# A one-core decoder layer: the loops of TensorE, VectorE, ScalarE and GpSimd written out in all three stages

## What is computed

```python
# 1: linear attention
Xn = _layernorm(X, ln_g, ln_b)
QKV = jnp.einsum('bsd,ed->bse', Xn, W_in)
Q, K, V = jnp.split(QKV, 3, axis=-1)
Q = _rotary(Q, ROT); K = _rotary(K, ROT)
A = jnp.sum(_l2norm(K) * V, axis=-2)
Y = A[:, None, :] * _l2norm(Q)
Y = jnp.einsum('bsd,ed->bse', Y, W_out); return Y + X
# 2: cross attention, 16 heads of 64; keys are the context's 64 rows and the latents' own 64
w = jnp.einsum('bhqd,bhkd->bhqk', q * scale, k * scale)
w = jax.nn.softmax(w.astype(jnp.float32), axis=-1).astype(q.dtype)
out = jnp.einsum('bhqk,bhkd->bhqd', w, v); return out @ Wo
# 3: mixture of 8 experts, the 2 best of each token
probs = jax.nn.softmax(jnp.einsum('bsd,de->bse', x, Wg) + bg, axis=-1)
topk_vals, topk_idx = jax.lax.top_k(probs, TOP_K)
h = jax.nn.gelu(jnp.einsum('bsd,edf->besf', x, W1) + b1[None, :, None, :], approximate=False)
y = jnp.einsum('besf,efd->besd', h, W2) + b2[None, :, None, :]
out = jnp.einsum('bse,besd->bsd', probs, y)
```

## Time and profile before

| | us |
|---|---|
| median of 3 runs | 1647.21 |
| lowest and highest | 1641.94 and 1647.63 |
| profiled execution: span from first to last instruction | 1682.3 |
| busy in it: TensorE, VectorE, ScalarE, GpSimd | 1437.9, 1337.9, 973.4, 971.4 |

### The profile page before, as it was taken

One profiled execution on the slowest core, in us unless ns is written; L12 is line 12 of the kernel. 1 busy time (PEld: TensorE's weight loads), 2 busy tenths in 40 slices (PEclk: granted clock), 3 DMA queues, 4 the chain that ended last, 5 costly groups with the idle time before them and its releaser, 6 DMA issues.

```text
span 1682.3 us, 41166 instructions
## 1 busy us (share of the span) xinstructions
PE 1437.9 (85%) x10381; PEld 1230.8 (73%) x10381; DVE 1337.9 (80%) x5130; ACT 973.4 (58%) x3763; POOL 971.4 (58%) x1485
## 2 busy tenths in 40 slices
PE   4689999999999999999999999999997498988950
PEld 3478787877777777878777777778885498988840
DVE  4478988888888898888888888988876577766757
ACT  2266666666656665666666566666664255544535
POOL 2355665666666666666666666666644245544458
PEclk7599999999999999999999999999998699999975
DMA  3000000000000000000000000000000666766647
GB/s 82 11 11 7 14 18 15 15 14 13 15 15 15 15 13 13 17 14 15 13 15 13 15 14 15 13 15 16 8 11 15 189 217 208 223 191 199 203 132 214
DMA packets 89529, 95.40 MB, mean 57 GB/s; under 512 B 12137, under 2 KB 75756, under 8 KB 89282
## 3 DMA queue, kind: packets, MB, share of 16 engines
q1 hardware_dynamic: 69714, 71.97, 14.8%
q0 software_dynamic: 8896, 17.20, 3.0%
q10 hardware_dynamic: 10800, 5.06, 1.2%
HBM read 71.88 MB, written 23.35 MB: 57 GB/s over the span
## 4 chain that ended last, share of the span: by engine, by line
DVE 37%; issue 25%; ACT 15%; PE 15%; DMA 3%; another core or an unknown queue 2%; POOL 1%; DVEq 1%; SPq 1%; ACTq 0%; POOLq 0%
ACT probs L622 14%; DVE neg_max L767 7%; DVE pT L779 3%; PE ps_t L1419 3%; DVE k_pick L824 2%; DVE x1s L854 2%; PE ps_u L1419 2%; DVE turned L810 2%; DVE l_hat L871 2%; DVE yT L834 1%; PE ps_a L1381 1%; DVE top_atf L950 1%; DVE st_z L845 1%; DVE st_x L862 1%
## 5 line engine op out<-in xcount | busy, mean ns | idle before, releaser
L622 ACT ACTIVATE probs<-ps_s,neg_max 128x128 f32<-128x128 f32 x1024 | 362.6, 366 | 433.2 <-DVE neg_max L767 432.2
L508 POOL TENSOR_TENSOR probs_n<-probs,inv_sum 128x512 f32<-128x512 f32 x256 | 265.5, 1037 | 150.7 <-DVE inv_sum L773 148.6
L1265 PEld LDWEIGHTS ps_s<-kvT,u_sb 128*128 128x128 f32 x2048 | 255.3, 192 | 48.7 <-issue 44.9
L1265 PE MATMUL ps_s<-kvT,u_sb 128*128 128x128 f32 x2048 | 281.5, 281 | 3.2 <-issue 3.2
L1278 PE MATMUL ps_o<-value_w,tT 128*128 128x128 f32 x2048 | 261.8, 276 | 2.7 <-ACT tT L633 2.2
L1298 PE MATMUL ps_t<-pT,kv_rows 128*128 128x512 f32 x512 | 262.3, 594 | 0.8 <-DVE pT L779 0.8
L1278 PEld LDWEIGHTS ps_o<-value_w,tT 128*128 128x128 f32 x2048 | 244.7, 192 | 6.8 <-ACT tT L633 4.1
L570 POOL DMA_INDIRECT y_rows<-wvT,f_id x144 | 146.4, 1017 | 169.9 <-DVE wvT L1179 124.9
L520 POOL DMA_INDIRECT x_rows<-routed,pos_i x128 | 136.3, 1065 | 132.0 <-DVE pos_i L1003 100.3
L1313 PE MATMUL ps_u<-lT_hi,score_hi 128*128 128x256 f32 x512 | 184.5, 360 | 27.4 <-DVE lT_lo L893 21.1
L622 ACT ACTIVATION_READ_ACCUMULATOR probs<-ps_s,neg_max 128x1 f32 x1024 | 207.6, 203 | 0.0
(11 more groups left out here) (246 smaller groups left out, 3453.2 us busy)
## 6 DMA issues: line engine op xcount, KB each, us to landing
u_sb<-in_expert_w SPq DMA_DIRECT2D x45, 578.0 KB
tT<-in_expert_w SPq DMA_DIRECT2D x27, 578.0 KB
f_x<-x_rows SPq DMA_DIRECT2D x72, 130.0 KB
tT<-y_rows SPq DMA_DIRECT2D x32, 256.0 KB, 3.7
x_raw<-in_x SPq DMA_DIRECT2D x64, 64.0 KB, 1.8
c_raw<-in_ctx_in SPq DMA_DIRECT2D x128, 32.0 KB, 2.0
out<-u_sb ACTq DMA_DIRECT2D x16, 256.0 KB, 3.0
y_rows<-wvT,f_id POOLq DMA_INDIRECT x144
```

The source lines that it names most:

```text
L508: nc.gpsimd.tensor_tensor(probs_n[:, sl], probs[:, sl], inv_sum[:, sl, :].rearrange("p (u o) -> p u o", o=1).to_broadcast([P, UP, P]), ALU ...
L622: last = nc.scalar.activation(probs[:, sl, j], ps_s[sl][:, j * P:(j + 1) * P], ACT.Exp, bias=neg_max[:, sl, j:j + 1], accum_out=sums[:, sl ...
L1265: last = nc.tensor.matmul(ps_s[sl][:, j * P:(j + 1) * P], u_sb[:, c // 2, BT * p + b, h:h + 2].rearrange("p h s -> p (h s)"), kvT[:, c, 1 ...
```

## The change

`periods` no longer has a loop: all 74 periods are written out on every engine, SyncE among them. `turns` no longer has a loop either and is used by all engines in stages two and three; the old one lives on as `rolled_turns`, which SyncE alone uses for the expert tiles. No instruction that computes on data is added, removed or moved. What goes are the branches, the loop registers and the register arithmetic ahead of waits and addresses; what comes is a longer instruction stream for each engine.

```diff
         def periods(eng, period):
 
-            lo = 6
-            fours = (NT - 6 - lo) // 4
-            hi = lo + 4 * fours
-            for t in range(FIRST, lo):
+            for t in range(FIRST, LAST + 1):
                 period(t, t % 4)
-            with eng.Fori(0, fours) as i:
-                for step in range(4):
-                    period(i * 4 + (lo + step), (lo + step) % 4)
-            for t in range(hi, LAST + 1):
-                period(t, t % 4)
-
-        def turns(eng, n, step, by, tail=0):
+
+        def turns(n, step, by):
+
+            for i in range(n):
+                step(i, i % by)
+
+        def rolled_turns(eng, n, step, by, tail=0):
...
-            turns(sp, NF, ffn, W_RING, W_RING)
+            rolled_turns(sp, NF, ffn, W_RING, W_RING)
...
-            turns(sp, NZ, last_in, RING)
+            turns(NZ, last_in, RING)
...
-            turns(pool, NF, ffn, W_RING)
+            turns(NF, ffn, W_RING)
...
-            turns(dve, NF, ffn, W_RING, W_RING)
+            turns(NF, ffn, W_RING)
...
-            turns(pe, NF, ffn, W_RING, W_RING)
+            turns(NF, ffn, W_RING)
```

More of the change, by code:

```diff
@@ L583, in last @@
                     rstd(e_mv[:, o, :, 1], e_ve[:, o], e_rs[:, o], eps_ln, e_moments, ZT * g, e_eps, e_rstd, g - 1)
-            turns(pool, NZ, last, RING)
+            turns(NZ, last, RING)
             last(NZ, 0)
@@ L708, in _ @@
             upper_weights(0, 0)
-            turns(act, NF, ffn, W_RING, W_RING)
+            turns(NF, ffn, W_RING)
             def last(g, q):
@@ L720, in last @@
                               e_out[:, q % 2]).then_inc(s_out[q % 2], 16)
-            turns(act, NZ, last, RING)
+            turns(NZ, last, RING)
         @block.vector
@@ L1209, in last @@
                     nc.vector.scalar_tensor_tensor(e_nm[:, o], e_mv[:, o, :, 0], -1.0, e_rs[:, o], ALU.mult, ALU.mult).then_inc(e_nm_done, 1)
-            turns(dve, NZ, last, RING)
+            turns(NZ, last, RING)
             last(NZ, 0)
```

## The result

| | before | after |
|---|---|---|
| median | 1647.42 us (1641.94 to 1648.0, 4 runs) | 1604.34 us (1603.82 to 1608.02, 4 runs) |
| ratio, 95% interval | | 0.9749 (0.9729 to 0.9768) |
| the profiled execution | span 1682.3 us | 1608.02 us, span 1606.1 us |
| stretch between the first row maxima of periods 6 and 58 | 998.5 us | 959.6 us |
| 56 expert tiles, `f_id` to `f_id` | 233.0 us | 196.6 us |

The account below looks back on a forecast made before the run. The prediction took VectorE's in-order stream, with its hand-over to ScalarE's exponentials, to bound the looped periods. Gains of 30.8 + 0 + 0 + 0.9 + 0.5 = 32.2 us off 1647.2 gave 1615.0 us, range 1603 to 1631.

Parts of the forecast that it names:

- The 12 jumps: VectorE's jumps back between the 13 turns of the looped periods: 2.57 us each, 30.8 us gained by removing them.
- Register arithmetic: Register instructions in the looped periods: removing them gains 0, bounds 2 us of loss and 1 us of gain.
- the test by period 5: Written-out period 5 takes 18.64 us against 18.60 looped, taken to show that register arithmetic in the periods costs nothing.
- Late pieces of code: Fetching the longer straight stream of the periods: 0 cost expected, upper bound 18 us.
- The rival: Late pieces of code all along the written-out periods, leaving 18 us of gain, 1629 us; chance 0.10.
- What the others' jumps cost: Jumps of the other four engines in the periods: nothing beside VectorE's, which explain the whole lengthening of the period.
- The expert tiles: Jumps removed among the expert tiles: 0.9 us gained, bounds nothing to 26 us.
- the expert tiles fall to the written-out pace: Rival: looped expert tiles go from 4.16 to 3.69 us each, 26 us more gain, 1589 us; chance 0.08.
- The last sum: Two ordinary jumps removed in the last sum: 0.5 us gained, between 0 and 1.
- I assume that this distance stays: The profiled span's 35.1 us above the median of the runs was assumed to remain after the change.
- Slower by code among the tiles: Rival: code fetches come late among the expert tiles, where DMA engines are busy, costing 72 us, 1687 us; chance 0.05.

Follow-up runs that it names:

- E2: Kernel before with the periods written out on TensorE, ScalarE, GpSimd and SyncE, VectorE still looped; first chip: 1696.18 us, ratio 1.003.
- E1: Kernel before with the periods written out on VectorE alone, every other loop kept; first chip: 1650.34 us, ratio 0.9759.
- E7: Kernel before with VectorE's loop at eight periods a turn instead of four, six turns in place of 13; second chip: 1629.74 us, ratio 0.9908.
- E3: Kernel before with the periods written out on all five engines, loops over expert tiles and last groups kept; first chip: 1656.79 us, ratio 0.9799.
- E11: Changed kernel with two already met waits added on VectorE ahead of each period's first row maximum; third chip: 1605.16 us, ratio 0.974.
- E12: Kernel before with the periods written out on all engines but TensorE; third chip: 1610.02 us, ratio 0.9773.
- E4: Kernel before with only the expert tiles written out, on all engines but SyncE; first chip: 1663.03 us, ratio 0.9829.
- E10: Kernel before with only the expert tiles written out, on all engines but SyncE; third chip: 1643.02 us, ratio 0.9975.
- E9: Changed kernel unchanged, run again on the third chip: 1603.88 us, ratio 0.9733.
- E5: Changed kernel unchanged, run again on the second chip: 1604.31 us, ratio 0.976.
- E6: Changed kernel with SyncE's loop over the expert tiles written out too; second chip: 1603.48 us, ratio 0.9751.
- E8: Changed kernel with four no-operations meant for VectorE ahead of each first row maximum, which did not get into the program; second chip: 1605.19 us, ratio 0.9769.

## Why the prediction was right, and where it fell short

**The 12 jumps, 30.8 us: right.** Four readings agree: the row is gone after, it stays in E2, E1 brings 35.5 us on its own (with VectorE's register arithmetic in it), and E7 keeps 5 jumps and 13.1 us of it.

**Register arithmetic, 0: wrong, and the largest error.** The written-out period is 18.42 us (E3 and E11: 18.41), the looped one 18.61: 52 x 0.184 = 9.6 us. My bounds were 2 us of loss and 1 us of gain. That the range still held the result was luck: its lower end had 10 us of spread that was meant for the expert tiles and the runs. The step that failed is the test by period 5, the last before the loop. The row maximum that ends it already stands in VectorE's loop, and ahead of it TensorE enters its own loop, which makes the scores late. The runs tell the two shares apart: period 5 takes 18.50 us where VectorE alone is looped (E2), 18.56 where TensorE alone is (E12), and 18.64 with all. Period 4, in the same trace, is free of both. Its first row maximum:

```profile
153.66 0.69 DVE L767 TENSOR_REDUCE neg_max<-ps_s 128x4 f32<-128x512 f32 x1
```

With the 172.10 of the earlier trace rows that is 18.44 us, which would have told it. E1 shows that the gain belongs to VectorE: 18.37 us with it alone written out, while E2, with the rest written out, stays at 18.67.

Where in the period it lies is read, not isolated. Counted from the row maximum of one quarter to the next, a looped period goes 4.88, 4.38, 3.72, 5.62 us, a written-out one 4.87, 4.31, 3.73, 5.52: the loss is in the second quarter and in the fourth. The chain ahead of the row maximum that ends the second quarter, before:

```profile
372.05 0.29 DVE st_x L862
372.34 0.03 issue
372.37 0.02 DVEq L312
372.39 0.04 issue
372.43 0.07 DVE mv_x L867
372.50 0.05 issue
372.55 0.02 DVEq L766
372.57 0.04 issue
372.61 0.70 DVE neg_max L767
```

and after:

```profile
386.16 0.29 DVE st_x L859
386.45 0.03 issue
386.48 0.02 DVEq L312
386.50 0.04 issue
386.54 0.06 DVE mv_x L864
386.60 0.04 issue
386.64 0.70 DVE neg_max L764
```

From `st_x` to `neg_max` it is 0.56 us looped and 0.48 written out. The step ahead of `mv_x`, L312, is a wait for VectorE's own result, so the sequencer can't run ahead, and what it does next lies bare between two short instructions. "DVEq L766" is the wait for ScalarE's exponentials, which the changed kernel has too (L763). What is longer is the way to it: in the loop the trace has a register instruction of 0.04 us (L765) between `mv_x` and L766.

The fourth quarter loses its time at its very end, ahead of the first row maximum of the next period. Before, and after:

```profile
363.05 0.28 DVE L893 TENSOR_TENSOR lT_lo<-kvT,l_upper 128x128 fp32r<-128x128 f32 x1
363.35 0.69 DVE L767 TENSOR_REDUCE neg_max<-ps_s 128x4 f32<-128x512 f32 x1
```
```profile
358.78 0.28 DVE L890 TENSOR_TENSOR lT_lo<-kvT,l_upper 128x128 fp32r<-128x128 f32 x1
358.99 0.69 DVE L764 TENSOR_REDUCE neg_max<-ps_s 128x4 f32<-128x512 f32 x1
```

TensorE's scores come at the same point in both, 0.18 us behind the start of `lT_lo`, by the updates of their semaphore. From there to the row maximum it is 0.11 us looped (before, E2, E4, E10) and 0.02 written out (after, E1, E3, E9, E11, E12; the middle one of 51 periods each). What stands in the longer gap is a register instruction of 0.04 us (L766): it waits for the scores itself and works out the count of the next wait, and only then can the row maximum be issued. E1 and E12 have the short gap with TensorE looped, E2 the long one with TensorE written out, so it is VectorE's own.

"The arithmetic runs on the sequencers while the datapaths work" holds, by these rows, only where the sequencer is ahead of its engine; behind a wait that ends last the arithmetic lies bare. E11's waits stood ahead of the score wait and cost nothing. Not tried: the looped kernel with the two waits ahead of the row maximum exchanged, so that the arithmetic stands ahead of the scores.

**Late pieces of code, 0: right, nearly.** 52 x 18.423 = 958.0 us stand against 959.6 measured: 1.6 us, mostly in six periods of 18.6 to 18.8 us (26, 27, 37, 46, 48 and 49). They are the same six in E3, E5, E6, E8 and E9, and others in E11, where VectorE's stream has two instructions more a period. So they hang on the place in the stream. The rival had 14 us and an upper bound of 18. The price is this small though q8, the queue I had taken for TensorE's, now moves all the time. The queues from 340.6 to 414.3 us of the changed kernel, four periods:

```profile
q8 instruction: 4, 0.07, 0.4%
...
q14 instruction: 6, 0.05, 0.3%
```

Before, q14 had 5 packets in a turn and q8 stood still. So straight code on all engines costs in q14 about what one engine's loop cost. What differs, as I read it, is when: along a straight line the code is there before it is needed, behind a taken branch it is fetched only once the engine has got there. VectorE's branch before is at 418.18 us, the next packet of 8192 bytes starts at 419.2, and the next instruction (of registers) runs at 421.0. This is what the Trainium skill says in "Runtime: NRT & Kernel Launch", section "Instruction fetch mechanics"; the 2.8 us between the branch and the next instruction agree.

**What the others' jumps cost, 0: right with all removed, wrong by its reason.** I said the lengthening was all VectorE's. It was, because 0.3 to 0.4 us of TensorE's jump lay under 2.6 us. Take VectorE's alone and 4 to 5.4 us come up (E1, E12). The change removed both, so the sum was not touched; for the smaller change it would have been.

**The expert tiles, 0.9 us: right on two chips, far off on the first.** On the third chip, the time from the first scatter of rows to the last is 250.0 us with all written out (E9) and 251.7 with looped tiles (E12): 1.7 us. E10's gain against the kernel before is 5.0 us, of which 3.3 are not located, since no profile of the kernel before is from that chip. The rival "the expert tiles fall to the written-out pace" took 4.16 - 3.69 us a tile for an effect of the loop. The pace did fall to 196.6 / 56 = 3.51 us, but looped tiles run at 3.55 too. My own reason, that the waits by "remote" are no branch, held on the third chip, yet E4 shows up to 25 us of gain on a chip that has them.

**The last sum, 0.5 us:** it takes 62.0 us from the last tile's `f_id` to the end, 61.7 before. No gain can be seen.

**"I assume that this distance stays": wrong, without harm.** The 35.1 us between span and median were the expert tiles of a slower execution, most likely of another chip. The periods that carry the sum hardly differ (998.5 to 1000.8 us looped, in the profile before, E4 and E10; 958.8 to 959.6 written out, on all three chips), so a difference worked out in them could be taken over.

**Slower by code among the tiles: wrong.** The change's tiles take 3.51 us each at 243 GB/s and a DMA share of 0.80, and VectorE waits by "issue" there hardly at all.

The sum again, with what was measured: on the third chip the stretch gave 998.7 - 959.0 = 39.7 us (E10 to E9) and the tiles up to 5.0 (E10, whose last sum is looped). That makes 44.7 us where 44.1 were measured between medians (1647.98 - 1603.88). The 39.7 are the jumps, 31.0 in E10, where the forecast had 30.8; the register arithmetic, 52 x (18.609 - 18.411) = 10.3, forecast at 0; and the late pieces, 1.6 the other way: 31.0 + 10.3 - 1.6 = 39.7. In the first pair the stretch gave 38.9 of the 43.1 us; the other 4.2, where the forecast had 1.4, are not located.

## What to carry to other kernels

Look in the list of waits for "issue" rows whose count is the number of turns less one: there an engine fetches its own loop again, and the price is that of a jump (2.6 us here), not of an instruction, so a longer body with fewer turns buys part of it for less code (E7: 7 of 12 jumps, 16 of the 39 us of the stretch). Take jumps off the engine that all others wait for first, and expect the next engine's to come up from underneath (E1, E12). In a loop, look also for register arithmetic behind the wait that ends last: it cost some 0.09 us there, while two more instructions ahead of that wait cost nothing (E11). To test a loop against straight code take a written-out period that touches neither end of the loop, and compare like parts of a span (here 52 periods) when whole runs come from different chips.

## What the runs showed of the hardware that was not expected

- **Not each loop is fetched again.** VectorE's body of some 430 recorded instructions a turn was, with 5 packets a turn on q14; q8 stood still during TensorE's turns of some 1130 from the third turn on, and the jumps that remained in E1 and E12 cost 0.3 to 0.4 us.
- **The same looped tiles take 198.8 us on two chips and 236 to 242 on another** (E7 and E12 against E1 to E3; 233 in the profile before), in E3 and E12 with the same instruction counts, a granted clock of 0.98 against 1.00 and a DMA share of 0.65 against 0.79. The loss comes in stalls of about 2.5 us. Written-out tiles there take 220.4 us (E4). The cause is open.
- **Straight code is close to free:** 52 periods of it on all engines cost 1.6 us, with 62 more packets on q8 and 19 on q14 over the whole kernel.
- **Fewer jumps beside it made VectorE's no cheaper:** in E2 its jumps took up to 3.2 us, against 2.8 before, and the stretch was 9.0 us longer.
